# A filtered gather-scatter pass of a graph network: the third message part on POOL, a message buffer of seven steps, and gathers two spans ahead

## The reference

```python
Wxh = x @ Wl.T + bl
h = jax.nn.silu(rbf @ Wf1.T + bf1)
f_ij = h @ Wf2.T + bf2
msg = f_ij * Wxh[j]
agg = jax.ops.segment_sum(msg, i, num_segments=x.shape[0])
y = x + agg
```

## Time and profile before

| | us |
|---|---|
| median of 3 runs | 9108.44 |
| lowest and highest | 9102.78 and 9114.54 |
| span of the profiled execution | 9113.9 |
| the filtered pass in it, first to last instruction | 4543 to 6299 |

### The profile page before, as it was taken

The page is one execution under the profiler, slowest core; times in us unless marked ns, Lnnn a source line. Parts: engine busy times, 40 slices in busy tenths (PEclk is TensorE's granted clock), DMA queues, the critical chain, the costliest instruction groups (busy, mean ns, idle before and its releaser), DMA issues. The chain is left out here.

```text
span 9113.9 us, 313494 instructions
## 1 busy us (share of the span) xinstructions
PE 7609.2 (83%) x101781; PEld 6597.8 (72%) x101781; DVE 6856.6 (75%) x13795; ACT 5224.4 (57%) x12664; POOL 3311.2 (36%) x3201
## 2 busy tenths in 40 slices
PE   6688888888888888887577877784799998899998
PEld 3466666666666666666477777774799997799998
DVE  3476676766766767666699999999788887677777
ACT  2344444444444444444477777774677775688887
POOL 5777777777777777775000000001000000000000
PEclk8899999999999999999799999998899999899999
DMA  4555555555555555554277777774233332466665
GB/s 152 159 164 179 166 174 175 156 181 167 168 175 168 177 171 157 183 168 135 66 187 188 187 187 188 189 188 103 108 129 129 129 129 79 93 127 130 129 130 109
DMA packets 889995, 1385.04 MB, mean 152 GB/s; under 512 B 385510, under 2 KB 738726, under 8 KB 877174
## 3 DMA queue, kind: packets, MB, share of 16 engines
q1 hardware_dynamic: 760470, 1100.18, 44.6%
q10 hardware_dynamic: 29376, 174.02, 5.3%
q0 software_dynamic: 100000, 109.00, 4.1%
HBM read 1086.88 MB, written 295.86 MB: 152 GB/s over the span
## 5 line engine op out<-in xcount | busy, mean ns | idle before, releaser
L796 POOL DMA_INDIRECT edge_rows<-f_rows,f_index x3125 | 3213.0, 1028 | 967.6 <-issue 950.3
L1084 ACT ACTIVATE f_msg<-ps,f_yew 128x64 f32<-128x64 f32 x4802 | 1052.7, 323 | 1446.3 <-PE ps L997 1372.4
L569 DVE TENSOR_TENSOR x_sel<-iotab,x_pairs 128x1792 bf16<-128x1792 bf16 (+1 forms) x1372 | 1172.6, 855 | 207.2 <-issue 196.3
L1333 PE MATMUL ps<-x_msg,x_sel 128*128 128x192 bf16 x9604 | 1184.4, 246 | 2.6 <-issue 2.4
L1687 ACT ACTIVATE x_msg<-ps 128x384 bf16<-128x384 f32 (+1 forms) x2744 | 1016.0, 458 | 206.7 <-PE ps L1619 199.0
L1360 ACT ACTIVATE x_msg<-ps 128x768 bf16<-128x768 f32 (+1 forms) x1029 | 906.1, 915 | 351.0 <-PE ps L1314 300.5
L1012 PE MATMUL ps<-f_msg,f_ysel 128*128 128x192 bf16 x9604 | 986.8, 255 | 116.2 <-issue 116.1
L1905 PE MATMUL ps<-tab,x_hot 128*128 (+1 forms) x28812 | 958.6, 194 | 23.0 <-ACT x_hot L1966 9.0
L1905 PEld LDWEIGHTS ps<-tab,x_hot 128*128 128x128 bf16 x28812 | 929.7, 98 | 53.7 <-issue 46.2
L1012 PEld LDWEIGHTS ps<-f_msg,f_ysel 128*128 128x128 bf16 x9604 | 844.3, 99 | 141.8 <-issue 126.2
L1619 PE MATMUL ps<-tab,x_hot 128*128 (+1 forms) x9604 | 923.9, 248 | 19.9 <-ACT x_msg L1687 8.0
(11 more groups left out here) (190 smaller groups left out, 13508.4 us busy)
## 6 DMA issues: line engine op xcount, KB each, us to landing
x_row<-edge_row_dst SPq DMA_DIRECT2D x588, 448.0 KB, 4.9
edge_rows<-zeros ACTq DMA_DIRECT2D x204, 833.0 KB
f_piece<-edge_rows SPq DMA_DIRECT2D x343, 476.0 KB
f_yrow<-edge_row_src SPq DMA_DIRECT2D x686, 224.0 KB
x_row<-edge_row_src SPq DMA_DIRECT2D x98, 1568.0 KB, 6.3
x_f<-edge_rows SPq DMA_DIRECT2D x294, 476.0 KB, 3.7
edge_rows<-f_rows,f_index POOLq DMA_INDIRECT x3125, 2.4
x_row<-edge_row_dst SPq DMA_DIRECT2D x196, 224.0 KB, 3.4
```

Of the source, the lines that this page charges most:

```text
L569: return dve.tensor_tensor(sel[:, :, :].rearrange("p c (e two) -> p c e two", two=2), iotab[:, 0:columns].rearrange("p (e two) -> p e two" ...
L796: pool.indirect_dma_start(out=rowbuf, out_offset=bass.IndirectOffsetOnAxis(ap=index[:, j:j + 1], axis=0), in_=rows[:, j, :], in_offset=Non ...
L1084: i = act.activation(msg[g % 2][:, c, 0, :], got[g % 2][:, c * D:(c + 1) * D], ACT.Copy, scale=yew[h][:, lo + c:lo + c + 1])
L1333: i = pe.matmul(total[:, m * VW:(m + 1) * VW], sel[c // CG % 2][:, c % CG, m * P:(m + 1) * P], msg[:, p % RING, k, :, :].rearrange("p k d ...
```

## The change

POOL makes the third part of each message (`low_of_message` moves from VectorE to POOL, with the same counters). `msg` gets a place for each of the seven steps of a run in place of four. TensorE begins with two gathers and then issues `gather(s+2)` ahead of `scatter(s)`. VectorE's order in a run becomes `whole_message(s)`, `first(s+2)`, `rest_of_message(s)`, `second(s)`. `whole_message(s)` waits for the scatter of span s-4 and no longer for that of s-2; so that this wait passes in the first run, the counter `x_sum` starts three steps higher (`SPARE`). POOL does its `collect` of a group after the first run of the next group.

```diff
+        SPARE = 3
...
-                msg = sbe("msg", [P, 4 * CG, V])
+                msg = sbe("msg", [P, RUN * CG, V])
...
+                def parts_of(s):
+                    return msg[:, SPANS[s][0] * CG:SPANS[s][1] * CG, :]
+                def scattered(eng, t, more):
+                    reach(eng, x_sum, t, more + SPARE)
...
# second, on VectorE
-                            reach(dve, x_sum, t, steps(s - 2)[1])
+                            scattered(dve, t, steps(s - 2)[1])
# whole_message, on VectorE
-                            reach(dve, x_sum, t, steps(s - 2)[1])
+                            scattered(dve, t, steps(s - 4)[1])
...
                                 rest_of_message(t, s)
-                                if s + 1 < 4 or not last:
-                                    second(t, i, s + 1)
-                                low_of_message(t, s)
+                                second(t, i, s)
...
# POOL
+                        def low_of_message(t, s):
+                            lo, hi = steps(s)
+                            part = parts_of(s)
+                            reach(pool, x_rest, t, hi)
+                            settle(pool)
+                            pool.tensor_tensor(part[:, :, 2 * D:3 * D], part[:, :, D:2 * D],
+                                               upper_of(part[:, :, D:2 * D]), ALU.subtract).then_inc(x_msg.sem, hi - lo)
+                        def run(t):
+                            for s in range(4):
+                                low_of_message(t, s)
...
-                            with loop(pool, 0, GW) as g:
+                            with loop(pool, 0, RUNS - 1) as r:
+                                run(step_of(pool, 0, r))
+                            with loop(pool, 0, GW - 1) as g:
+                                run(step_of(pool, g, RUNS - 1))
+                                run(step_of(pool, g + 1, 0))
                                 collect(g)
+                                with loop(pool, 1, RUNS - 1) as r:
+                                    run(step_of(pool, g + 1, r))
+                            run(step_of(pool, GW - 1, RUNS - 1))
+                            collect(GW - 1)
...
# TensorE
-                                if s + 1 < 4:
-                                    gather(t, s + 1, e + steps(s + 1)[0] * WROW)
+                                if s + 2 < 4:
+                                    gather(t, s + 2, e + steps(s + 2)[0] * WROW)
                                 elif follow is not None:
-                                    gather(t, 4, follow)
+                                    gather(t, s + 2, follow + SPANS[s - 2][0] * WROW)
                                 scatter(t, s, last and s == 3)
...
-                            gather(0, 0, 0)
+                            for s in range(2):
+                                gather(0, s, steps(s)[0] * WROW)
```

More of the change, by code:

```diff
@@ L1819, in whole_message @@
                             reach(dve, x_got, t, hi)
-                            reach(dve, x_sum, t, steps(s - 2)[1])
+                            scattered(dve, t, steps(s - 4)[1])
                             settle(dve)
-                            dve.tensor_tensor(msg[:, b * CG:e * CG, 0:D].rearrange("p (b c) d -> p b c d", c=CG),
+                            dve.tensor_tensor(parts_of(s)[:, :, 0:D].rearrange("p (b c) d -> p b c d", c=CG),
                                               psum[:, b * 512:e * 512].rearrange("p (b e) -> p b e", e=512)[:, :, 0:CG * D]
@@ L1829, in rest_of_message @@
                             lo, hi = steps(s)
-                            part = msg[:, SETS[s][0] * CG:SETS[s][1] * CG, :]
+                            part = parts_of(s)
                             reach(dve, x_whole, t, hi)
@@ L1834, in rest_of_message @@
                                 .then_inc(x_rest.sem, hi - lo)
[L1836 to L1842, removed]
                         def run(t, i, last=False):
@@ L1858, in _ @@
                                 first(0, 0, s)
-                            second(0, 0, 0)
                             with loop(dve, 0, RUNS - 1) as r:
@@ L1918, in scatter @@
                                     o = pe.matmul(sums[c // 2][:, c % 2 * V:(c % 2 + 1) * V], sel[:, b * CG + c, :],
-                                                  upper_half(msg[:, b * CG + c, :]),
+                                                  upper_half(msg[:, (SPANS[s][0] + j - lo) * CG + c, :]),
                                                   start=False, stop=last and j == hi - 1 and (c % 2 == 1 or c == CG - 1))
@@ L1940, in _ @@
                         with under(pe, 0):
-                            for c in (x_got, x_sum):
-                                pe.sem_inc(c.sem, CREDIT)
+                            pe.sem_inc(x_got.sem, CREDIT)
+                            pe.sem_inc(x_sum.sem, CREDIT + SPARE)
                             cleared()
-                            gather(0, 0, 0)
+                            for s in range(2):
+                                gather(0, s, steps(s)[0] * WROW)
                             rounds(0)
@@ L1973, in taken @@
                         def taken(g):
-                            act.wait_ge(x_sum.sem, g * NW + x_sum.at(CREDIT + NW))
+                            act.wait_ge(x_sum.sem, g * NW + x_sum.at(CREDIT + SPARE + NW))
                             act.wait_ge(x_acc.sem, g * 3 + x_acc.at(CREDIT))
@@ L1997, in filter_pass @@
                 c_.base += CREDIT + GW * NW
+            x_sum.base += SPARE
             x_acc.base += CREDIT + GW * 3
```

## The result

The changed kernel takes 8945.35 us (median, 8939.81 to 8954.38) against 9109.46 us for the kernel before, a ratio of 0.9822 with a 95% interval of 0.9810 to 0.9834: 164 us less. The forecast was 8982 us with a range of 8930 to 9240. The profiled span fell from 9113.9 to 8952.6 us, and nearly all of it in the filtered pass.

The account below looks back on a forecast made before the run. VectorE was taken as the bound, TensorE close behind. Runs saving 165 us less 39 us lost at group changes made 126 us less: 8988 us for a profiled execution, 8982 for the median, range 8930 to 9240.

Parts of the forecast that it names:

- The turns: Filtered pass: POOL and VectorE alternate whole instructions, only the product runs beside POOL; run 15.75 us against 17.43, 165 us less.
- the 1.5 of three spans in four: Sign on VectorE: `first` would show about 1.5 us instead of 0.67 in three of four spans.
- the product is held: Rival: VectorE's product also waits for POOL, nothing overlaps, run 19.16 us, kernel 9317 us; chance 0.13.
- nothing is held: Rival: no VectorE instruction waits for POOL, TensorE becomes the bound, kernel 8899 us; chance 0.06.
- The size of the term: POOL's full-span third-part instruction: 2.03 us long, occupying what it shares with VectorE for 1.84 us.
- The row loads: SP's row loads queue behind pairs and filter but just fit, at most 0.7 us late, inside the gather's slack.
- a rival at 0.8 us a run: Rival: rows come late, slots stretch by about 0.8 us a run, kernel 9060 us; chance 0.10.
- The sign that I had named: The forecast was to fail if VectorE waits for the row loads; no size given.
- TensorE two ahead: Gathers issued two spans ahead end 1.0 to 2.7 us before their product, removing the 0.96 us wait a run.
- The buffer: Seven-step message buffer lets the product go on without scatter(s-2); without it POOL's lateness would add a wait, unsized.
- The group change: Sums, activations and gather delay the product 4 us; with the collect 6 us against 3.0, 39 us more at 13 changes.

Follow-up runs that it names:

- e1: Changed kernel plus four POOL subtractions after the pass's last collect, VectorE idle: 1.68 us with bf16 view, 2.09 float, 0.93 half-size; one run, 8963 us.
- e3: Changed kernel with SP issuing the load of row(h+1) before pairs(h) and filter(h): 8898 us, ratio 0.9776 to the kernel before.
- e5: Changed kernel with the third part back on VectorE, gathers two ahead and seven-step buffer kept: ratio 0.9934 to the kernel before.
- e2: Changed kernel with TensorE's gathers only one span ahead of the scatters again: 9347 us, ratio 1.0272 to the kernel before.
- e7: Changed kernel with the message buffer of four steps again, product waiting for the scatter of s-2: ratio 0.9942 to the kernel before.
- e4: Changed kernel with ScalarE making the next group's upper one-hot of span 2 before copying the sums: 8901 us, ratio 0.9777 to the kernel before.

## Why the prediction was right

**The turns.** Right. POOL and VectorE take whole instructions in turns; in ordinary runs it is `first` that is held, and the product is not: 1.09 and 0.62 us beside POOL. (`rest` and `second` are over before POOL gets its turn; only the collect at a change holds `rest`, 1.94 us.) The full-size `first` averages 1.04 us over the pass and not the 1.5 of three spans in four, because VectorE reaches it later where the product has waited or is a full one. Over the pass the full products take 1.087 us each on average, 1.086 before. The rival "the product is held" is excluded by this, "nothing is held" by `first`'s 1.57 us. The Trainium skill, "SBUF — State Buffer", section "Who interferes with whom", had named the case of at most one SBUF input, outside the two-port modes, as free of contention; the trace agrees, with these 1.087 us, for an instruction whose other input is in PSUM.

**The size of the term.** The price of POOL's instruction was mis-sized: 2.03 us taken, 1.68 measured (e1), occupancy 1.43 for 1.84. Three full spans make it 1.23 us a run, so the floor is 15.75 - 1.23 = 14.52; e3 shows 14.51. The 1.43 is read from the changed kernel itself; with the 1.49 from e1 the floor would be 14.70. I had bounded the price from below by the float instruction and from above by the one short bf16 one; for an operand of another type the float row was no lower bound.

**The row loads.** Put at nothing in the forecast, and wrong there. The prediction worked out that the rows just fit, called the margin thin, and gave lateness a chance of 0.10 as a rival at 0.8 us a run. With the shorter run it came true: 15.09 - 14.51 = 0.58 us a run and 54 us over the intervals (e3, by taking it away). Longer landing times may be part of it, 4.9 us before and 5.5 in the pass of the changed kernel. The sign that I had named, VectorE waiting for the row loads, is the wrong place to look: VectorE waited 12 us for them, 9 before; the delay went through ScalarE's 158 us and TensorE. ScalarE is also busier than the prediction had it, 12.82 us a run and not 12.5.

**TensorE two ahead.** The gain of 0.96 us a run is right by e5 (16.43 against 17.43). That the price without it, once POOL makes the message, is 5 us a run (e2) I had not seen; I checked that the new order works and not what the old one would do.

**The buffer.** Right in kind: the four-step buffer adds a wait for the scatter, 0.8 us a run (e7).

**The group change.** Right in place, too small: the surcharge rose by 5.3 us instead of 3.0. The chain sums, activations, gather is as written (product due at 5237.0 by its predecessor, started at 5244.13, 7.1 us late, where I had 4). Two reasons fit the rows: slots are shorter than I had laid out, so it is due earlier, and the gather ran at the lower clock, 4.96 us, where I had added only 0.4 for it. How the 2.3 us divide between them was not tested. e4 shows that ScalarE's order makes 3.9 us of the surcharge.

In sum: 227 us from the runs where 165 were forecast, 69 us lost at the changes where 39 were; 158 against 126. Three errors are behind the difference: POOL's shorter instruction gave about 120 us more (1.23 us in 97 runs), the late rows took 54 to 56 of it, and the changes took 30. That they cancel in good part is luck; the time came out nearer to the forecast than its terms.

## What to carry to other kernels

When work moves to an engine that waits for its turn, the consumer's order matters more than the work: with the same POOL code the kernel was 1.8% faster or 2.7% slower than before, by whether TensorE had its next gather ahead of the scatter. When limits lie close together (here row loads at 15.0 us, turns at 14.5 and TensorE at 14.1), removing one shows little; take away the other first and test again. After a loop turn is written out for the sake of order, look at the instruction queue of the DMA view: here the written-out run cost more than the wait it removed.

## What the runs showed of the hardware

A POOL subtraction of 896 float elements took 2.09 us with a float second operand and 1.68 us with a strided bf16 view in its place. A VectorE product with one operand in PSUM ran undelayed beside POOL (1.087 us on average), while a one-hot comparison of 1792 elements went from 0.67 to 1.57 us. Writing TensorE's run of 343 matmuls out a third time inside a loop raised the instruction packets in the pass from 7 to 131 and cost 8.4 us on average once in each group (14.53 to 22.91 us in the last interval). At a group change TensorE stood idle for 1.83 and 3.25 us with only the clearing of the banks (0.73 us) between; the clock granted for the next gather was 0.50, the lower level. In ordinary runs five gathers behind a standstill of 1.55 to 2.77 us had a mean granted clock of 0.63 to 0.69, in part the lower level, and took 4.12 to 4.57 us instead of 2.61.
